# A single-core two-layer gated cross-attention and expert block: the hand-kept order of each engine's steps is replaced by another

## The chip, the cores and the metric

The kernel runs on one NeuronCore of a Trainium2 chip. The metric is the device time of one execution in microseconds (us), the median of several runs. The core has five instruction streams that run side by side and meet at semaphores: PE (TensorE, the matmuls), DVE (VectorE), ACT (ScalarE), POOL (GpSimd) and SP (SyncE, which here issues nearly all DMA transfers).

## The reference

Eight batch elements, each with 256 tokens of 128 numbers (`x`) and a context of 512 tokens of 96 numbers (`ctx`). Four blocks follow each other, each on a layer-normed `x`, with a gate in front of what is added:

```
x = x + tanh(g_xattn[0]) * cross_attention_8_heads_of_64(layernorm(x), ctx)
x = x + tanh(g_ffn[0])   * (self_attention_16_heads_of_8(layernorm(x)) + top2_of_8_experts(layernorm(x)))
x = x + tanh(g_xattn[1]) * cross_attention_16_heads_of_8(layernorm(x), ctx)
x = x + tanh(g_ffn[1])   * top2_of_8_experts(layernorm(x))
```

The four blocks of one batch element depend on each other; the eight elements do not, so the kernel keeps several of them in flight.

## The kernel before

**Stages and steps.** The stages are X (first cross-attention), F (self-attention with the first experts), K (keys and values of the second cross-attention), B (the second cross-attention) and C (the second experts). A step is named by stage, name, batch element b (0 to 7) and a running number k. Nearly every step on PE fills one bank of PSUM, or a pair of banks, and one step on ACT or DVE, the drain, reads it out.

The steps that matter below, with their lines: `ls` (DVE, L1063 and L1066: mean and variance), `rs` (POOL, L1273 and L1274: the reciprocal standard deviation), `xh` (DVE, L1073: normalise), `ln` (PE, L692: transpose, drained by ACT at L923), `qp` (PE L697, two drains on ACT, L937 and L938: queries of X), `kp` (PE L702, ACT L943 and L944: keys of X, two steps for each element), `vp` (PE L708, ACT L947: values of X), `mx` (PE L714, DVE L1105: the largest score of each row of X, eight steps of one wide reduction each), `mT` (PE L720), `e` (PE L730 and L734, ACT L953: scores again and their exponentials), `pv` (PE L743). In stage K, `ctx` (SP L597) loads the context `cTK`, `kk` (PE L772) makes keys and `vv` (PE L826, DVE L1177) values. In F and B, `qk` (PE L765) makes queries (F: and keys), `sp` (POOL L1309 to L1311) splits them into three bf16 parts, `sw` (SP L604, L608) stores the parts to DRAM, `sr` (SP L619, L622) loads them back in another layout (`q8`, `k8`), `mx8` (PE L841 and L847, DVE L1220 and L1225) finds the row maxima, `mT8` (PE L852) transposes them, `mw` and `mr` (SP L652, L657) send them through DRAM into a row of `q8`, and `e8` (PE L866, ACT L996) makes the exponentials, which `pv8` (PE L878) uses.

On POOL there are three steps that occur once: `sets` (L1259, L1262: five memsets of constants into `k8` and `v8`, and two small products that wait until all weights have landed), `bo` (L1251: two bias rows times a gate) and `pick` (L1254: a selection matrix that the first `e` needs). The drains of `vv`, and the loads `sr`, wait for `sets`.

**What sets the order.** The order on each engine is written out in a table, `TURN_OF` (L80 to L105): one string for each engine, in which each letter names a kind of step and takes the next one of that kind. A planner (`schedule`, L332 to L384) walks through these strings, gives each PE step its PSUM banks, and puts filler matmuls (L686) ahead of a PE step where it reckons a long idle time. The instruction streams are then emitted in that order, with a semaphore wait wherever a step needs another engine's. An engine never overtakes: a step that waits holds up all that stands behind it on that engine. For SP this means that a load whose condition is not yet met holds up all later transfers.

**Array shapes on PE.** A step uses the PE array whole, or in halves or quarters of its rows or columns. The table `MODE` (L47 to L50) says which of five shapes a step has (0 whole, 1 row halves, 2 and 3 column halves and quarters, 4 row quarters).

```
MODE = {("X", "mx"): 1, ("X", "e"): 1, ("X", "out"): 1, ("F", "mx8"): 1, ("F", "e8"): 1, ("B", "mx8"): 1, ("B", "e8"): 1,
```

Of the kernel before, what the change touches and what calls it, by code (L numbers as in the profile page):

```python
# [7 lines left out]
ACT = mybir.ActivationFunctionType  # L8
# [81 lines left out]
    "DVE": "abpacccbcccccpdeeccccfcgccchiiikajbkkmkmmmmmmmncdeclecccfgaccchoioqiikrkjkbkmmmmmmmmssnssssssssssssssdtccceclcec"  # L90
           "fcgohoiqciikkrkkplpujuammvmmmmmmsnssswsxsssssssyszsbszszzotAoAcAqccdeerfcgAchcapiuiuicckkkvwxpkmmmmsssssymjmmmnz"
           "sbssszlsssssdzzssAtAeceAccAfcgchocciioqikrkckakmmmpmjmpumlumbssmnsssssssssssssvsdwtxeecycczfcgzzzacAhiAiooiAckqc"
           "ckjrbAkmmmmmumpkupmmnssvswsssssssslssxssstyozozzzdAceecqfAgcrhcAiicAikcckkcpumkmmmsumsspmsmmsnjsssssslsssssvwtdx"
# [1294 lines left out]
```

## Time and profile before

| | before |
|---|---|
| median of 3 runs | 726.27 us (725.82 to 726.75) |
| the profiled execution, its own time | 733.98 us |
| its span, from the first to the last instruction | 732.2 us |
| PE busy | 666.7 us, 91% of the span |
| DVE busy | 515.4 us, 70% |
| ACT busy | 402.4 us, 55% |
| POOL busy | 385.8 us, 53% |
| mean granted TensorE clock | 0.968 of full speed |
| the chain that ended last, by engine | PE 53%, DVE 26%, ACT 6%, POOL 5%, DMA 4% |

Times in the rows are counted from the span's start. An engine's row gives its idle time just before, in brackets, and what ended it. A matmul of fp32 data shows as two records for each instruction, so a step of four matmuls reads as x8. The profiled execution is 7.71 us longer than the median of the runs without a profile, so differences are taken against its own time and then carried over to the median.

### The profile page before, as it was taken

Reading aid. Unit: us, or ns where it says so; the run is one execution under the profiler, and the core shown is the slowest. Engines: PE = TensorE matmul, PEld = TensorE weight load, DVE = VectorE, ACT = ScalarE, POOL = GpSimd, SP = SyncE. Lnnn points to the kernel's source line nnn. Section 1 sums busy time; section 2 is a strip of 40 time slices with the busy share of each in tenths; the row PEclk is TensorE's granted clock in tenths of the full one; section 3 lists DMA queues with packets and bytes.
Section 4 is the critical chain, followed back from the end, with each engine's and each line's share of the span. In section 5 each row is a group of like instructions: output and inputs, shape, how many; then the busy total and the mean of one; then the engine's idle time right before and its main releaser. Section 6 shows DMA issues by size and latency. Waiting matters only on the chain.

```text
span 732.2 us, 14403 instructions
## 1 busy us (share of the span) xinstructions
PE 666.7 (91%) x5766; PEld 347.3 (47%) x5766; DVE 515.4 (70%) x1018; ACT 402.4 (55%) x574; POOL 385.8 (53%) x535
## 2 busy tenths in 40 slices
PE   6898998998989899988999998999999999999984
PEld 4454554543445454543445454546445543544542
DVE  2505658698558965778868889777479979957636
ACT  1464556446734676426673586476744666376540
POOL 5465675781454547563538746573648625234041
PEclk9899999999898999989999999999999989999998
DMA  6040400511091010820145124240060031000000
GB/s 179 22 95 5 101 3 9 119 24 45 10 161 34 2 45 9 168 33 3 46 99 104 54 51 86 56 99 10 1 130 26 20 78 45 1 20 8 2 1 15
DMA packets 58338, 36.92 MB, mean 50 GB/s; under 512 B 4984, under 2 KB 56288, under 8 KB 58272
## 3 DMA queue, kind: packets, MB, share of 16 engines
q1 hardware_dynamic: 57728, 35.74, 22.2%
q8 instruction: 45, 0.74, 0.4%
q10 hardware_dynamic: 544, 0.26, 0.1%
q14 instruction: 21, 0.17, 0.1%
HBM read 21.07 MB, written 14.93 MB: 49 GB/s over the span
## 4 chain that ended last, share of the span: by engine, by line
PE 53%; DVE 26%; ACT 6%; POOL 5%; DMA 4%; issue 3%; SPq 1%; DVEq 0%; POOLq 0%; ACTq 0%
PE psum L878 7%; PE psum L730 6%; PE psum L743 5%; DVE mx8B L1225 5%; DVE mx8F L1220 5%; PE psum L834 5%; PE psum L866 4%; DVE mxA L1105 3%; PE psum L847 2%; PE psum L702 2%; PE psum L803 2%; PE psum L708 2%; ACT probB L996 2%; PE psum L815 2%; PE psum L761 1%
## 5 line engine op out<-in xcount | busy, mean ns | idle before, releaser
L1225 DVE TENSOR_REDUCE mx8B<-psum 128x2 f32<-128x1024 f32 x112 | 131.6, 1216 | 15.1 <-PE psum L847 14.2
L996 ACT ACTIVATE probB<-psum 128x1024 f32<-128x1024 f32 x112 | 110.7, 1028 | 25.5 <-PE psum L866 19.9
L953 ACT ACTIVATE probX<-psum 128x1024 f32<-128x1024 f32 x64 | 65.5, 1023 | 54.8 <-PE psum L734 54.2
L1105 DVE TENSOR_REDUCE mxA<-psum 128x2 f32<-128x1024 f32 x64 | 76.5, 1217 | 25.2 <-PE psum L714 24.9
L1220 DVE TENSOR_REDUCE mx8F<-psum 128x4 f32<-128x1024 f32 x56 | 66.2, 1219 | 21.9 <-PE psum L841 21.5
L730 PE MATMUL psum<-qA,kA 64*128 64x256 f32 x512 | 76.9, 393 | 1.0 <-ACT mrow L926 0.5
L996 ACT ACTIVATE probF<-psum 128x1024 f32<-128x1024 f32 x56 | 56.7, 1026 | 21.1 <-PE psum L866 17.8
L743 PE MATMUL psum<-probX,vX 128*64 128x256 f32 x512 | 63.8, 393 | 0.7 <-ACT probX L953 0.3
L1316 POOL TENSOR_TENSOR prodC<-prodC 128x256 f32<-128x256 f32 x28 | 20.3, 727 | 73.7 <-DVE prodC L1197 73.7
L878 PE MATMUL psum<-probB,v8B 128*9 128x256 f32 x896 | 56.0, 392 | 0.3 <-ACT probB L996 0.2
L1292 POOL TENSOR_TENSOR sums<-probX 128x512 f32<-128x512 f32 x32 | 40.6, 1267 | 21.4 <-ACT probX L953 21.3
L730 PEld LDWEIGHTS psum<-qA,kA 64*128 64x128 f32 x512 | 40.3, 189 | 23.5 <-issue 5.5
L866 PE MATMUL psum<-q8B,k8B 49*128 49x256 bf16 x448 | 43.6, 284 | 5.2 <-ACT probB L996 2.1
L743 PEld LDWEIGHTS psum<-probX,vX 128*64 128x64 f32 x512 | 34.6, 139 | 25.6 <-issue 8.6
L847 PE MATMUL psum<-k8B,q8B 48*128 48x512 bf16 x224 | 41.2, 384 | 6.0 <-DMA q8B<-q_dB 3.3
L1295 POOL TENSOR_TENSOR sums<-sums,probX 128x512 f32<-128x512 f32 x32 | 40.6, 1269 | 10.7 <-ACT probX L953 8.4
L1300 POOL TENSOR_TENSOR sums<-sums 128x512 f32<-128x512 f32 x15 | 19.0, 1267 | 43.5 <-DVE sums L1114 43.5
L1296 POOL TENSOR_TENSOR sums<-sums,probX 128x512 f32<-128x512 f32 x32 | 40.6, 1268 | 2.5
L734 PE MATMUL psum<-mrow,pick 64*128 64x256 bf16 x256 | 35.8, 271 | 0.0
L878 PEld LDWEIGHTS psum<-probB,v8B 128*9 128x9 f32 x896 | 22.4, 92 | 28.1 <-issue 6.7
L866 PEld LDWEIGHTS psum<-q8B,k8B 49*128 49x128 bf16 x448 | 15.5, 97 | 42.5 <-ACT probB L996 12.8
L834 PE MATMUL psum<-weF,xTF 128*128 128x512 f32 x64 | 34.6, 622 | 0.8 <-ACT probB L996 0.5
(254 smaller groups left out, 1368.0 us busy)
## 6 DMA issues: line engine op xcount, KB each, us to landing
k8B<-k_dK SPq DMA_DIRECT2D x14, 384.0 KB, 6.8
k_dK<-partsK SPq DMA_DIRECT2D x7, 384.0 KB, 2.6
q8F<-q_dF SPq DMA_DIRECT2D x14, 192.0 KB, 4.3
k8F<-k_dF SPq DMA_DIRECT2D x14, 192.0 KB, 5.0
q8B<-q_dB SPq DMA_DIRECT2D x14, 192.0 KB, 4.0
k_dK<-partsK SPq DMA_DIRECT2D x7, 256.0 KB, 2.9
cTX<-in_ctxT SPq DMA_DIRECT2D x8, 192.0 KB, 2.6
cTK<-in_ctxT SPq DMA_DIRECT2D x8, 192.0 KB, 2.5
```

The source lines that it names most:

```text
L730: mm(ps[:, 512 * i + SEQ * c:512 * i + SEQ * (c + 1)], kA[half_i, h, (2 * f + c) * P:(2 * f + c + 1) * P], qA[half_i, h, :], start=True, s ...
L743: last = mm(ps[64 * i:64 * i + 64, 0:SEQ], vX[:, c, h * XD:(h + 1) * XD], prob[s][(2 * k + c // 2) % SLOTS[s]][:, o:o + SEQ], start=(c == ...
L834: last = mm(ps, xT[s][:, t * P:(t + 1) * P], we[s][:, f * 512:(f + 1) * 512], start=True, stop=True)
L847: last = mm(ps[:, KV * i:KV * (i + 1)], q8[s][b % TURNS[s]][64 * i:64 * i + KROWS, p, t * P:(t + 1) * P], k8[s][b % TURNS[s]][64 * i:64 * ...
L866: last = mm(ps[:, 512 * i + SEQ * c:512 * i + SEQ * (c + 1)], k8[s][b % TURNS[s]][64 * i:64 * i + MROWS, p, (c0 + c) * P:(c0 + c + 1) * P] ...
L878: last = mm(ps[32 * i:32 * i + D8 + 1, 0:SEQ], v8[s][:, c, h, :], prob[s][(NPAIR * KEYS[s] // SEQ * b + u) % SLOTS[s]][:, o:o + SEQ], star ...
L953: nc.scalar.activation(prob[s][k % SLOTS[s]][:], ps, ACT.Exp, scale=float(XD) ** -0.5).then_inc(done["ACT"], 1)
L996: nc.scalar.activation(prob[s][(units * b + k) % SLOTS[s]][:], ps, ACT.Exp, scale=float(D8) ** -0.5).then_inc(done["ACT"], 1)
L1105: nc.vector.tensor_reduce(mxA[:, t, h:h + 65:64], ps.rearrange("p (i n) -> p i n", i=2), AX.X, ALU.max, negate=True).then_inc(drained, 1)
L1220: nc.vector.tensor_reduce(mx8[s][:, :, 2 * k:2 * k + 2].rearrange("p t i -> p i t"), ps.rearrange("p (i t n) -> p i t n", i=2, t=QT), AX.X ...
L1225: nc.vector.tensor_reduce(mx8[s][:, t, 2 * p:2 * p + 2], ps.rearrange("p (i n) -> p i n", i=2), AX.X, ALU.max, negate=True).then_inc(drain ...
L1292: engine.tensor_tensor(sums[:, h], p[:, :, 0, :], p[:, :, 1, :], ALU.add).then_inc(S["X"]["psum"], 1)
```

## The change

The steps are the same: each engine has as many steps as before, of the same kinds (937 on PE, 571 on DVE, 505 on ACT, 228 on POOL, 104 on SP). Only the five strings of `TURN_OF` differ, nearly everywhere, and with them the banks and the fillers that `schedule` works out. Two lines of the table stand for all:

```
@@ -78,30 +78,30 @@
 TURN_OF = {
-    "POOL": "dacebalffffffffggehijfafffjffffjjkggehlimajfnojffjfjffffkggheimjjjjkonfalfpfffffqqfqmggheqriojjfpnffjfjffakfflqq"
+    "POOL": "acedbalffffffffggehijajffffffffjjkggheimfaojjfffjffljffkgghneiamjjojfffjknpflffffqgghemqqioqrpjjaffjfjffffkfnlqq"
...
-    "SP": "abgaghbibacdefacdjbkeflhmcdaigjkbeflhmacjdngikbeflmhcadijkgbhefnilmacdjgkefbhilnmcjdkgoefnlmhijklngmnnnn",
+    "SP": "bagaghbbacdiefacbdjkeflmhiacdjkgefbhlmacjdnikgbeflhmiacdjgbkefhnlmcdiajkebgfhlmnicdjokengflmhijklngmnnnn",
```

**The start of POOL.** These are POOL's first rows behind the three short memsets, before the change. `veX` and `rstdX` are the step `rs` of element 0, and the memsets of `k8` and `v8` with the two products `bqm` are `sets`:

```order
L1259 MEMSET k8F 128x2048
L1259 MEMSET k8B 128x4096 x2
L1259 MEMSET v8F 128x288
L1259 MEMSET v8B 128x576
L1262 ISA
L1262 TENSOR_SCALAR bqmF<-mask,bqn 128x4
L1262 TENSOR_SCALAR bqmB<-mask,bqn 128x4
L1273 TENSOR_SCALAR veX<-mvX 128x2
L1274 TENSOR_TENSOR rstdX<-veX,nhalf 128x2
L1251 TENSOR_SCALAR boX<-boX,gates 128x128
```

The same place of POOL after the change:

```order
L1273 TENSOR_SCALAR veX<-mvX 128x2
L1274 TENSOR_TENSOR rstdX<-veX,nhalf 128x2
L1251 TENSOR_SCALAR boX<-boX,gates 128x128
L1251 TENSOR_SCALAR boB<-boB,gates 128x128
L1283 TENSOR_TENSOR xbX<-xin,boX 128x256
L1259 MEMSET k8F 128x2048
L1259 MEMSET k8B 128x4096 x2
L1259 MEMSET v8F 128x288
L1259 MEMSET v8B 128x576
L1262 TENSOR_SCALAR bqmF<-mask,bqn 128x4
L1262 TENSOR_SCALAR bqmB<-mask,bqn 128x4
L1254 TENSOR_TENSOR pick<-ident 128x512
```

The step `rs` of element 0, with `bo` and `xb` behind it, has moved ahead of `sets`; `pick` stands behind `sets` now.

**The start of PE.** PE's first steps behind the fillers, before the change (`vp`, `kp`, `ln`, `vv`, `qp`, `kp`, then the first `mx`):

```order
L708 MATMUL psum<-wvx,cTX 128x512 x2
L702 MATMUL psum<-cTX,wkx 128x512 x2
L692 MATMUL psum<-ident,xhX 128x128 x2
L826 MATMUL psum<-wv8B,cTK 128x128 x2
L697 MATMUL psum<-xTX,wqx 128x256 x4
L702 MATMUL psum<-cTX,wkx 128x512 x2
L714 MATMUL psum<-kAb,qAb 128x512 x2
```

The same place of PE after the change:

```order
L702 MATMUL psum<-cTX,wkx 128x512 x2
L692 MATMUL psum<-ident,xhX 128x128 x2
L697 MATMUL psum<-xTX,wqx 128x256 x4
L708 MATMUL psum<-wvx,cTX 128x512 x2
L714 MATMUL psum<-kAb,qAb 128x512 x4
L702 MATMUL psum<-cTX,wkx 128x512 x2
L714 MATMUL psum<-kAb,qAb 128x512 x4
```

The keys, the transpose and the queries have moved ahead of the values, the first two `mx` ahead of the second `kp`, and `vv` behind four `mx`. ACT drains in the matching order (`ln`, `kp`, `qp`, `vp`, `kp`), and DVE reduces six `mx` before its first drain of `vv`, with `ls` of element 1 behind the second.

**SP around the third load of the context for stage K.** Before the change, behind the loads of `q8F` and `k8F` of element 2 (`xin` is x of element 4, `k8B` the keys of B for element 1, `cTK` the context for K of element 2, `q_dB` and `q8B` the queries of B for element 1):

```order
L588 DMA xin<-in_x 128x2x128
L622 DMA k8B<-k_dK 48x8x512 x2
L597 DMA cTK<-in_ctxT 96x512
L604 DMA q_dB<-partsB 128x3x256
L604 DMA q_dB<-partsB 128x2x256
L604 DMA q_dB<-partsB 128x256
L619 DMA q8B<-q_dB 48x8x256 x2
```

The same place of SP after the change:

```order
L604 DMA q_dB<-partsB 128x3x256
L604 DMA q_dB<-partsB 128x2x256
L604 DMA q_dB<-partsB 128x256
L619 DMA q8B<-q_dB 48x8x256 x2
L597 DMA cTK<-in_ctxT 96x512
L652 DMA m_dF<-m8F 16x256
```

`k8B` and `xin` have moved ahead of the stores of element 2's F parts, and `cTK` behind `q8B`. On PE the step `kk` of element 2, which needs this `cTK`, stood 6 steps behind `qk` of B of element 1 and stands 19 steps behind it now.

## Rows read from the trace of the kernel before

**Rows 1.** The page, busy time of PE and its weight loads: share, instructions.

```profile
PE 666.7 (91%) x5766; PEld 347.3 (47%) x5766; DVE 515.4 (70%) x1018; ACT 402.4 (55%) x574; POOL 385.8 (53%) x535
```

**Rows 2.** Stretches: length, busy us of PE, PEld, DVE, ACT, POOL (instructions), PEclk, DMA, GB/s.

```profile
40.00:80.00 40.00, 37.78 (x280) 21.32 (x276) 15.53 (x32) 21.69 (x32) 24.90 (x26) 1.00 0.15 29
...
160.00:200.00 40.00, 36.69 (x343) 16.67 (x344) 28.97 (x41) 28.52 (x38) 12.99 (x17) 0.91 0.06 21
200.00:240.00 40.00, 35.99 (x296) 19.03 (x294) 27.60 (x58) 17.93 (x27) 20.00 (x29) 0.91 0.50 94
...
280.00:320.00 40.00, 34.79 (x253) 17.28 (x253) 24.92 (x56) 19.25 (x33) 26.57 (x41) 0.91 0.53 95
```

**Rows 3.** Timeline of the start: start us, us, engine, line, operation, tiles, count, idle before.

```profile
2.80 6.96 POOL L1259 MEMSET k8B<- 128x4096 bf16 x2
...
5.73 0.25 DVE L1066 BATCH_NORM_AGGREGATE mvX<-st6X 128x2 f32<-128x6 f32 x2
...
13.54 1.88 PE L708 MATMUL psum<-wvx,cTX 96*128 96x512 f32 x4
...
15.26 1.88 PE L702 MATMUL psum<-cTX,wkx 96*128 96x512 f32 x4
...
17.77 0.32 POOL L1262 TENSOR_SCALAR bqmF<-mask,bqn 128x4 f32<-128x4 f32 x1 [7.21 <-DMA weB<-in_weB]
...
18.64 0.72 POOL L1274 TENSOR_TENSOR rstdX<-veX,nhalf 128x2 f32<-128x2 f32 x1
...
19.40 0.65 DVE L1073 TENSOR_SCALAR xhX<-xin,mvX,rstdX 128x128 f32<-128x128 f32 x2 [13.42 <-POOL rstdX L1274]
...
20.20 0.66 PE L692 MATMUL psum<-ident,xhX 128*128 128x128 f32 x2 [3.06 <-DVE xhX L1073]
...
20.90 0.38 ACT L923 ACTIVATE xTX<-psum 128x256 f32<-128x256 f32 x1 [4.41 <-PE psum L692]
21.18 1.02 ACT L943 ACTIVATE kAb<-psum 128x1024 bf16<-128x1024 f32 x1
...
21.51 3.67 PE L697 MATMUL psum<-xTX,wqx 128*128 128x256 f32 x8
...
26.14 1.02 ACT L938 ACTIVATE qA<-psum 128x1024 f32<-128x1024 f32 x1
...
27.41 0.39 PE L714 MATMUL psum<-kAb,qAb 64*128 64x512 bf16 x2
...
27.84 2.36 DVE L1105 TENSOR_REDUCE mxA<-psum 128x2 f32<-128x1024 f32 x2 [3.44 <-PE psum L714]
```

**Rows 4.** The chain that ended last, in order of time: start us, us, what.

```profile
31.84 5.67 DVE mxA L1105 x5
...
501.51 1.73 PE psum L697 x8
```

**Rows 5.** Timeline of PE: two neighbouring steps of different array shape.

```profile
306.13 0.28 PE L734 MATMUL psum<-mrow,pick 64*128 64x256 bf16 x2
306.34 1.95 PE L743 MATMUL psum<-probX,vX 128*64 128x256 f32 x16
```

**Rows 6.** Timelines of SP, then PE, around `kk` of element 2.

```profile
212.11 0.34 SPq L597 DMA_DIRECT2D cTK<-in_ctxT  x1
...
218.16 2.08 PE L772 MATMUL psum<-cTK,wk8B 96*128 96x512 f32 x2 [3.54 <-DMA cTK<-in_ctxT]
...
221.00 1.06 PE L730 MATMUL psum<-qA,kA 64*128 64x256 f32 x4
```

**Rows 7.** Timelines of SP, then PE, around the first `mx8` of B, element 2.

```profile
303.84 1.29 SPq L619 DMA_DIRECT2D q8B<-q_dB  x2
...
315.28 0.61 PE L847 MATMUL psum<-k8B,q8B 48*128 48x512 bf16 x2 [3.28 <-DMA q8B<-q_dB]
...
316.25 3.66 PE L743 MATMUL psum<-probX,vX 128*64 128x256 f32 x16
```

**Rows 8.** Timeline of PE: the first `e8` of B, element 0.

```profile
181.06 0.40 PE L866 MATMUL psum<-q8B,k8B 49*128 49x256 bf16 x4 [1.31 <-DMA q8B<-m_dB]
```

More of the change, by code:

```diff
@@ L90 @@
[L90 to L93, printed above, removed]
-           "eeBfoogqyzrzzhzACiADDiDDikADkDkDkDsjssssussssuspAsssssstvwxylpzooqrzzzAEAFAFFAFFFFFuppuFFFFFvwFFxFyzzzzAAAAuuvwx"
-           "yzzzzGGHGGH",
@@ L101 @@
-    "POOL": "dacebalffffffffggehijfafffjffffjjkggehlimajfnojffjfjffffkggheimjjjjkonfalfpfffffqqfqmggheqriojjfpnffjfjffakfflqq"
-            "ggheimqjojjjaffkfflfqfffrnpggehiqqqamjjqofrjjlfffnfpkfffqggmhqiqojjqjjfffffkefrfflpnghmsoqjjqqjqrpjknmqqqqrnpqqq"
+    "PE": "baceddbddyydxdddexfaggggghghggcbhihjkkdbddedddedldmnpofpggbghgpggaphhsgsgssssbshsiqtcjkkeduduuduvuudvudluvdmddrv"
+          "newowfpggpzgAhpqpgsgsshsgssashsgBBtgBBBBcBbuBuBBBhBuBvBuiBBjuvCudkdubdkDvDdDdDrDuDEvlDDdnwmDpDDEDwpDdDEDdDpozypy"
+          "qEAfFeFgsgsgsssgsessGxHrtBBhBgBhuBuIaBuBvuBguBgBJBvuBBuvBuBhvBgwCbcKhDdDiDDwKDjDEDdDkDkDdEDDKDbDdElDDnmdEdzFKAod"
+          "yFedGpHfpyggpeqpIhsgsgsgsJBBhsgsgsBhBgsBBxbtbBBhBaKuBuiBuBvBuBBBcrKjCdkuevuukvDdDKDduKDdDvEDdDlwDdnmwDEDDdpeDdpD"
+          "DEDozDfApEpyFyFgsgssgshsgsgsBgBxqBsBhBgBGratBgbHBBhBuBhuBiBuBvBBucjCukuvIdkuvuJdDDvDdDbDdlKwmnDEDodDKDEdDKpDDdwq"
+          "pDEDdpeKzDsfAsyDgsEsesgssgspFytFhBgBGxHBBuhBugBuvuBgBrIuBvuBhBuBvugBvaBgBBJbCwcwKihjDdDkDDdDkDEDdDbDdEDdlKmdDnzp"
+          "DdADDEdDDypKfyeEKFpFesgsgsgsgsGsqBBhsgBgBgBshtBHBgBpBhBuoxBuBhBuBvuBiBuvCIjrJukuvukDvDDwDKDwDEDlDKNLznAKDOOoDDEp"
+          "DOpODMKOOEDBDpDBBPqOEBPFBQBByQBBFPRBBQOQBQBBpGBQBRPyCHRQQIxJRDDrDwDwKDDEDDzKSDEUDDKUDDTUEDUDKVUDWUEUWUWUWyVFyFUW"
+          "UWXGUWUWVHUWUWUWXVWIWKJKWWWXKKXFFGHIJYYYY",
@@ new lines @@
+    "DVE": "abccaccccpccbdpececccfcgccchiaiijkkkbkmmmmmmmmndeecccfcgccclhcoioqiirkkajkmmmbkmmmmmssnssssssssssssssdtcecceccfg"
+           "lochiiaiokcqrkkbcpupkujmmmmmmmmvwnslsssxsssssssysssszsztzzoAcoAdceqcefAgcrhccuAjcuapicipivkwxkkbmkmmmyssmmsmsszm"
+           "znszszssAssssssslAtdececAcAfcgcochoqaiciikckrbkupupkjmmmmmmmssssmsnlssssvsswsssssxtdececyfcgzzzozAhcciAiicAjcokq"
+           "krkcAmmmpammmmmpnuuksbsvwsssssxssslssssssytozzzoqzAdcecrecfcgcAhciciikckAAukpumpmmmmmssmssmsnsvswssksxjsssssstdy"
+           "lezeBozfogqzzArAChDjiiiADkDkDDDAskssDsussspsssusDsssksstvwxlpooyqzrzzzEAAFFFFFAFAFFFpupuFFFFvFwFFxyzzzzAAAAuuvwx"
+           "yzzzzGGHGGH",
@@ new lines @@
+    "ACT": "abcdboeafdfffofgffgfcbghgbddijkeffffffbgggaffbglhcdmmmnmmmnminmjkndefpffqlgffgfgfafcmmbgmmnhmnmmbrnrrrmrrsnirrjk"
+           "rrsrrrrsrrpslqedfffftdogfgmmuammnfmfnmvmnmgnfbcrgrrhrrrsrrrrsrrrbrsirrjspqktdeffduglfffgffgfvbbgoammhmnmcmdmnmrr"
+           "rmnrnrsrirrjkrrsrdrrrrprqsesfffgffflogfatfbgmgmhmnmcmmumnnmrrnvrrribjrsrrkrrsrrrrsdplerqrsfdffgftmomgfmnmfummngm"
+           "nmfnafvbhcgrrrrrrsrrbrirsjrkprqrrsrrsdedffffltgffgffgmmomgmmhunnmvmnmrnrrrrrrisrpxqrkrsrrrwsrrrysylzzAyzzztzyAzA"
+           "zuoArrrrvrrrprsrsrrrrBsrrCrDsDDDCDEtDDCDDDCDDuDEvDDDEEtuv",
@@ L103 @@
+    "POOL": "acedbalffffffffggehijajffffffffjjkggheimfaojjfffjffljffkgghneiamjjojfffjknpflffffqgghemqqioqrpjjaffjfjffffkfnlqq"
+            "ggeqhiajmojqffrjfjfkffffplgghnieqjmqqjqoffajrffjpklffnffmgghqeijoqqjqffffjrfffpfnljkgshmoqjqqjqjrjnpkmqqqqrpqqnq"
             "qrpt",
-    "SP": "abgaghbibacdefacdjbkeflhmcdaigjkbeflhmacjdngikbeflmhcadijkgbhefnilmacdjgkefbhilnmcjdkgoefnlmhijklngmnnnn",
+    "SP": "bagaghbbacdiefacbdjkeflmhiacdjkgefbhlmacjdnikgbeflhmiacdjgbkefhnlmcdiajkebgfhlmnicdjokengflmhijklngmnnnn",
```

14 lines of the change are left out of this document (removed).

## Prediction

> **What bounds the kernel now.** I read the page's busy shares first. PE is busy for 91% of the span [rows 1]. Next I read the stretches: from 40 us on PE works 35 to 38 of every 40 us, while DVE works 15 to 29 and ACT 18 to 29 [rows 2]. So from then on the kernel is a queue of PE work with short waits in it, and time is won in three ways: the queue starts earlier, its work gets cheaper, or a wait goes. The same rows show what a long wait costs besides itself: in three of the four stretches the mean granted clock is 0.91, which is 0.09 x 40 = 3.6 us of full-speed PE time lost, since the clock is at 1.2 instead of 2.4 GHz for a part of the stretch. Then I read the timeline of the start. The mean and variance of the first element are ready at 5.73 + 0.25 = 5.98, but POOL's `rs` ends at 18.64 + 0.72 = 19.36, since POOL stands in `sets`, at last until the weights have landed at 17.77 [rows 3]. DVE waits 13.42 us for it and PE 3.06 us, and PE then runs `ln` and `qp` at 1.2 GHz: the 8 records of `qp` take 3.67 us there against 1.73 us at 501.51 [rows 3, 4]. The first `mx` begins on PE at 27.41 and on DVE at 27.84; the eighth ends at 31.84 + 5.67 = 37.51 [rows 3, 4]. Last I looked for the longest waits of PE behind the start: 3.54 us for `cTK` at 218.16 and 3.28 us for `q8B` at 315.28 [rows 6, 7].
>
> **The start.** With `rs` ahead of `sets`, it runs from about 6.0 to 7.1 and `xh` is done before 8 (0.65 us). Now the fillers bound it: PE's first step begins at 13.54 as before, and that is `kp`; the step after it follows at 15.26 [rows 3]. The clock is full by then: the four records of `vp` take 1.88 us. `ln` took 0.66 us at 1.2 GHz, so some 0.4 at 2.4: to 15.7. ACT's copy takes 0.38 us (to 16.1), and PE starts `qp` 0.23 us behind it (21.51 against 20.90 + 0.38), at 16.3; at full clock it lasts 1.73 us, to 18.0. ACT meanwhile drains `kp` in two pieces of 1.02 us, from 16.1 to 18.1, then `qp` in two, to 20.2. The first `mx` follows 0.25 us behind that drain (27.41 against 26.14 + 1.02), at 20.4, and DVE 0.43 us later, at 20.85. That is 7.0 us earlier than 27.84. DVE bounds what follows until the eighth `mx`, and `ls` of element 1, some 0.8 us, now stands among them, so 7.0 - 0.8 = **6.2 us** remain at `mT`. By then PE's order holds the same steps as before, apart from one `ln` that moved behind `mT`. What could be late next: `sets` starts near 9.8, behind `bo` and `xb`, lasts about 9.7 us (its two largest memsets take 6.96) and ends near 20.1, as the weights have landed by 17.77; `pick` ends near 21. The first `e` needs `pick` after 31, and the first drain of `vv` stands behind six `mx`, near 29, so both have 8 us to spare and cost nothing. Without that cover each us of POOL would be a us of PE. Bounds of the start: 3.1 us (PE's wait alone) to 7.0.
>
> **Array shapes.** Two neighbouring PE steps of the same shape overlap by 13.54 + 1.88 - 15.26 = 0.16 us; of different shapes by 306.13 + 0.28 - 306.34 = 0.07 us [rows 3, 5]. A change of shape thus costs 0.09 us. Counted by `MODE` over the 937 steps of PE's order there were 482 changes and are 447, so 35 x 0.09 = 3.2 us of PE time go; PE is busy for 91%, hence **2.9 us** (0 where another engine ends the wait, 3.2 at most).
>
> **Two waits.** `cTK` for element 2 is issued at 212.11 behind 768 KB of `k8B` and PE waits 3.54 us for it [rows 6]. Now `k8B` goes out a whole stage earlier and `cTK` behind `q8B`, so it is issued some 8 us behind `qk`, but `kk` stands 19 steps behind `qk` instead of 6. Work between two steps is counted here and below as the sum of the steps between them in PE's order, each at the median duration that its kind has in this trace. That gives 13.2 us of PE work instead of 3.2, and eight of them are `mx8` of F, which DVE paces at over 1.1 us each. I count the wait as gone. The slow clock behind it took `e`'s first part from 0.6 to 1.06 us [rows 6]; of the stretch's 3.6 us I count 2.8, as part of the slow time fell into the wait. Together **6.3 us** (0 to 7.1). `q8B` of element 2 is issued at 303.84 behind `cTK` and `k8B`, and `mx8` waits 3.28 us [rows 7]. Now `cTK` goes behind it and PE has 22.3 instead of 17.4 us of work between `qk` and `mx8`. The cover grows by 4.9 us, more than the wait, so it goes as well, and with it the slow clock that took `pv` from 1.95 to 3.66 us [rows 5, 7]; I count 2.0 for the clock. Together **5.3 us** (0 to 6.9).
>
> **What is given back.** The trace of before can't show the waits of the new order. It shows what such a place costs: the row transfer of B's maxima held PE 1.31 us at 181.06 [rows 8], and the stretch lost 3.6 us of clock [rows 2], of which I count 3.2, so 4.5 us for the place. Covers have shrunk elsewhere: from `mT8` to `e8` of F there were 9.7 and 10.1 us of PE work for elements 1 and 4 and there are 6.8 and 7.2; of B, element 1, 8.0 and now 6.9, with the stores of K's parts put ahead of the row. I let one new place of 4.5 us come, and 3.1 us of waits too short to touch the clock: **-7.6 us**. Between none and five such places (0 to 22.5) I take the lower side, since the other covers of this kind lie between 5.7 and 7.6 us as before.
>
> **The sum.** 6.2 + 2.9 + 6.3 + 5.3 - 7.6 = 13.1 us off the profiled execution's 733.98, so 720.9; that execution stands 7.71 us above the median 726.27, and I carry the difference over: 726.3 - 13.1 = 713.2 us.
>
> **The rivals.** First, **the start alone**: PE time that is set free turns into waits for DVE and ACT, and as many long waits come as go. Then only the 6.2 us count: 720.1 us. For it: no term but the start is a chain that can be followed to its end in the rows; against it: both long waits have a named transfer that moved. The Trainium skill, Perfetto Trace Analysis, "Identifying the Most-Contended Engine", speaks for it: a high matmul share is no good measure of how near TensorE is to its limit, and the busy share of its weight loads is the better one. By it PE would have half its time to spare, since PEld is at 47% [rows 1], and cheaper PE work would bring little. The long waits that PE's rows show, few between 40 and 80 us (37.78 of 40 busy), speak against that reading here.
>
> Second, **all of it stays**: no new long wait comes, and the whole 20.7 us are kept: 705.6 us. For it: fillers that the planner puts where it reckons a long wait stood at two places within PE's order and stand at none now. Against it: at 181.06 and 315.28 there was no filler, and the waits came.
>
> Third, **slower**: the rows of maxima come late. Each of the 14 trips from `mT8` over `mw` and `mr` to `e8` must fit under the PE work between them. If DVE reads `mT8` 1.5 us late, or `mw` stands behind a store of K's parts, the trip of about 6 us no longer fits, and the place costs 4.5 us. Five places eat the 20.7 us; from there on it is slower. Six cost 27.0 us: 726.3 + 27.0 - 20.7 = 732.6 us. For it: at 181.06 a cover of 5.7 us was too short. Against it: of the 14 trips only this one held PE for over a us before, and most covers are unchanged.
>
> Fourth, **nothing**: the start's gain is lost again within the first element, because POOL's sums or DVE bound it until PE's queue fills. Then it is about 726 us. Against it: between 40 and 80 us POOL works 24.90 and DVE 15.53 of 40 us, PE 37.78 [rows 2].
>
> **How the numbers follow.** The forecast of 713.2 gets 0.52, the start alone 0.21, all of it 0.12, slower 0.09, nothing 0.06. The likeliest is the forecast, with a range of its own from 708 to 718. To hold 8 in 10 the range must reach the start alone, with a little for its bounds (3.1 instead of 6.2 would be 723.2), and most of the way to the second rival: 704 to 722, which leaves out the slower case and nothing. A difference of 0.2% (1.5 us) is about what a measurement of this kernel can tell from no change. Faster by more: 0.52 + 0.21 + 0.12 = 0.85; within: 0.06; slower by more: 0.09.
>
> **What would show it.** In the profile of the changed kernel, `rstdX` should end near 7 us, the first `qp` last 1.7 us, the first `mx` on DVE start near 20.9 and the eighth end near 31.3; POOL's `pick` should end before PE reaches `e`. `kk` of element 2 and the first `mx8` of B of element 2 should begin without a wait for a transfer, and the stretches around them show a clock of 1.00. New stretches with a clock near 0.91 would show what is given back, and the row ahead of each names the wait. The prediction is wrong if `pick` or a drain of `vv` holds PE in the start, if PE's idle time behind 40 us grows by more than some 10 us, or if late rows of maxima show up at several `e8`.

## Result and profile after

The changed kernel takes 701.49 us (median, 700.24 to 702.48) against 726.51 us for the kernel before beside it: a ratio of 0.966 with an interval of [0.963, 0.968], or 25.0 us off. The forecast was 713.2 us with a range of 704 to 722. So the sign is right, and the gain is about twice the forecast and lies outside the range.

The profiled execution of the changed kernel takes 700.24 us, its span 698.4 us. Two rows of its page answer to [rows 1] and to the last line of the table of before: busy us, share of the span and instructions of each engine, and the chain that ended last.

```profile
PE 647.8 (93%) x5762; PEld 341.9 (49%) x5762; DVE 520.7 (75%) x1018; ACT 403.8 (58%) x574; POOL 385.9 (55%) x535
...
PE 53%; DVE 32%; POOL 6%; issue 4%; ACT 3%; DMA 1%; SPq 0%; DVEq 0%; POOLq 0%; ACTq 0%
```

PE is busy for 18.9 us less than in the profiled execution of before, and idle for less too. The stretches that answer to [rows 2], with one more (the columns are those of [rows 2], the granted clock is third from the end):

```profile
40.00:80.00 40.00, 38.34 (x270) 20.98 (x268) 19.07 (x44) 19.12 (x27) 25.14 (x31) 1.00 0.11 30
160.00:200.00 40.00, 37.22 (x410) 18.03 (x410) 31.80 (x66) 28.92 (x41) 15.78 (x24) 1.00 0.33 76
200.00:240.00 40.00, 37.99 (x366) 20.68 (x358) 35.04 (x49) 23.33 (x35) 23.21 (x26) 1.00 0.23 59
280.00:320.00 40.00, 37.13 (x293) 19.60 (x296) 34.02 (x65) 20.16 (x29) 29.32 (x36) 1.00 0.39 70
...
440.00:480.00 40.00, 37.52 (x324) 19.53 (x325) 33.93 (x46) 21.62 (x30) 26.64 (x33) 0.96 0.16 48
```

The three stretches that stood at 0.91 stand at 1.00. Between the start and the last 60 us only the stretch from 440 to 480 falls below 1.00, to 0.96. The timeline of the start, which answers to [rows 3]:

```profile
6.46 0.72 POOL L1274 TENSOR_TENSOR rstdX<-veX,nhalf 128x2 f32<-128x2 f32 x1
...
14.38 1.88 PE L702 MATMUL psum<-cTX,wkx 96*128 96x512 f32 x4
...
16.09 0.38 PE L692 MATMUL psum<-ident,xhX 128*128 128x128 f32 x2
...
16.95 1.99 PE L697 MATMUL psum<-xTX,wqx 128*128 128x256 f32 x8 [0.47 <-ACT xTX L923]
...
19.99 1.04 POOL L1254 TENSOR_TENSOR pick<-ident 128x512 bf16<-128x512 f32 x1
...
21.41 2.36 DVE L1105 TENSOR_REDUCE mxA<-psum 128x2 f32<-128x1024 f32 x2 [13.59 <-PE psum L714]
...
29.19 2.35 DVE L1105 TENSOR_REDUCE mxA<-psum 128x2 f32<-128x1024 f32 x2
```

The first `mx` starts on DVE at 21.41 in place of 27.84, and the eighth ends at 31.54 in place of 37.51, so `mT` stands 5.9 us earlier. The two steps of the long waits, `kk` and the first `mx8` of B of element 2, answer to the PE rows of [rows 6] and [rows 7]. They have no bracket now, which means no idle time ahead of them:

```profile
213.88 1.02 PE L772 MATMUL psum<-cTK,wk8B 96*128 96x512 f32 x2
...
296.70 0.81 PE L847 MATMUL psum<-k8B,q8B 48*128 48x512 bf16 x4
```

**Where the time went.** Executions of the kernel before differ among themselves. I therefore took its profile once more.

> The kernel before, unchanged, profiled a second time. Its first profiled execution took 733.98 us against a median of 726.5, the changed kernel's 700.24 against 701.5, so the two traces differ by 33.7 us and the medians by 25.0. If the long waits and the stretches at 1.2 GHz of the first trace belong to the order of the steps, this one shows the same waits (3.5 us at the third kk, 3.3 us at q8B of the third element), the same five slow stretches behind 160 us and a time near 734. If the slow stretches come and go between executions while the waits stay, it takes about 726 with two or three slow stretches fewer (each some 3 us).

That execution took 723.92 us, with a mean clock of 0.986 where the first profile had 0.968 (733.98 us). Both long waits are there again, while low clock stands at three places behind 160 us where the first profile had five. So, as far as two executions show, the waits belong to the order, and the low clock comes and goes:

```profile
213.71 1.34 PE L772 MATMUL psum<-cTK,wk8B 96*128 96x512 f32 x2 [3.58 <-DMA cTK<-in_ctxT]
...
308.92 0.39 PE L847 MATMUL psum<-k8B,q8B 48*128 48x512 bf16 x2 [2.36 <-DMA q8B<-q_dB]
```

Over the executions of before in three later comparisons, the 11 with a mean clock of 0.976 or less took 731.4 us on average, and the 13 at 0.985 or more 724.5 us. The first profile was thus an execution with more low clock than usual, and the second one is nearer to the typical one. The span is PE's busy time, its idle time and 9.4 us behind its last instruction. Split further by the clock records of the trace (full speed is 2.4 GHz, the low level 1.2; the fourth row is an estimate, the busy time less half of what fell into low clock):

| us | before, first profile | before, second profile | after |
|---|---|---|---|
| span | 732.2 | 722.1 | 698.4 |
| PE busy | 666.7 | 658.0 | 647.8 |
| of it at the low level | 36.7 | 13.6 | 3.2 |
| PE's work, were all of it at full clock | 648.3 | 651.1 | 646.2 |
| PE idle ahead of its instructions | 56.0 | 54.7 | 41.3 |

Against the second profile the span fell by 23.7 us: 13.4 us of waits, 5.2 us of clock ((13.6 - 3.2) / 2) and 4.9 us of work. These three add up to 23.5 us. The work row has a flaw: the clock records of the second profile and of after begin at 13 to 14 us, so the slow fillers of the start count there as full, and in the first profile only some of them do; that is why 648.3 and 651.1 differ with the same instructions. From the end of these fillers to the fillers ahead of the last `ln`, PE's work at full clock is 634.0, 634.8 and 629.3 us. The forecast had all three kinds in it; the experiments ask which of its terms were worth what.

### The profile page after: what moved, and what is told of

It is laid out like the page before. It is cut to its first block, busy times and chain, and to the rows that moved or that the text cites. A ratio compares the mean times of both kernels' runs of the same rounds, so it can differ in the third digit from the quotient of the medians.

```text
span 698.4 us, 14395 instructions
## 1 busy us (share of the span) xinstructions
PE 647.8 (93%) x5762; PEld 341.9 (49%) x5762; DVE 520.7 (75%) x1018; ACT 403.8 (58%) x574; POOL 385.9 (55%) x535
## 4 chain that ended last, share of the span: by engine, by line
PE 53%; DVE 32%; POOL 6%; issue 4%; ACT 3%; DMA 1%; SPq 0%; DVEq 0%; POOLq 0%; ACTq 0%
DVE mx8B L1225 8%; PE psum L730 6%; PE psum L743 6%; PE psum L878 6%; PE psum L834 5%; DVE mxA L1105 3%; PE psum L866 3%; PE psum L708 3%; PE psum L803 3%; DVE mx8F L1220 2%; PE psum L847 2%; PE psum L697 2%; POOL sums L1300 2%; PE psum L702 2%; PE psum L841 2%
## 5 line engine op out<-in xcount | busy, mean ns | idle before, releaser
L996 ACT ACTIVATE probB<-psum 128x1024 f32<-128x1024 f32 x112 | 110.3, 1029 | 15.2 <-PE psum L866 14.7
L730 PE MATMUL psum<-qA,kA 64*128 64x256 f32 x512 | 75.5, 387 | 2.2 <-DVE mx8F L1220 0.6
L743 PE MATMUL psum<-probX,vX 128*64 128x256 f32 x512 | 62.1, 385 | 1.0 <-DVE mx8B L1225 0.7
L878 PE MATMUL psum<-probB,v8B 128*9 128x256 f32 x896 | 53.6, 380 | 0.8 <-DVE prodF L1197 0.4
L866 PE MATMUL psum<-q8B,k8B 49*128 49x256 bf16 x448 | 42.2, 273 | 5.0 <-DMA q8B<-m_dB 1.2
L1316 POOL TENSOR_TENSOR prodF<-prodF 128x256 f32<-128x256 f32 x32 | 23.3, 728 | 34.7 <-DVE prodF L1197 34.7
```

The costliest lines, as they stand in the source:

```text
L730: mm(ps[:, 512 * i + SEQ * c:512 * i + SEQ * (c + 1)], kA[half_i, h, (2 * f + c) * P:(2 * f + c + 1) * P], qA[half_i, h, :], start=True, s ...
L743: last = mm(ps[64 * i:64 * i + 64, 0:SEQ], vX[:, c, h * XD:(h + 1) * XD], prob[s][(2 * k + c // 2) % SLOTS[s]][:, o:o + SEQ], start=(c == ...
L866: last = mm(ps[:, 512 * i + SEQ * c:512 * i + SEQ * (c + 1)], k8[s][b % TURNS[s]][64 * i:64 * i + MROWS, p, (c0 + c) * P:(c0 + c + 1) * P] ...
L878: last = mm(ps[32 * i:32 * i + D8 + 1, 0:SEQ], v8[s][:, c, h, :], prob[s][(NPAIR * KEYS[s] // SEQ * b + u) % SLOTS[s]][:, o:o + SEQ], star ...
L996: nc.scalar.activation(prob[s][(units * b + k) % SLOTS[s]][:], ps, ACT.Exp, scale=float(D8) ** -0.5).then_inc(done["ACT"], 1)
L1316: link("X", engine.tensor_tensor(pr_[:, 0:2 * P], pr_[:, 0:2 * P], pr_[:, 2 * P:], ALU.add))
```

## Experiments

The ratios are to the kernel before in the same comparison; 0.001 is 0.73 us. Where two kernels of different comparisons are set against each other, I subtract their ratios; by the intervals, such a difference is good to about 3 us either way, and to 4 us for e2_rest.

**The parts alone, in the old order.** e1_start is before with the rearranged start: the first 20 steps of PE, 13 of DVE, 7 of ACT and 5 of POOL in the order of after. e2_rest is the counterpart, after with the start of before. PE's part of e1_start:

```diff
-L708 MATMUL psum<-wvx,cTX 128x512 x2
 L702 MATMUL psum<-cTX,wkx 128x512 x2
 L692 MATMUL psum<-ident,xhX 128x128 x2
-L826 MATMUL psum<-wv8B,cTK 128x128 x2
 L697 MATMUL psum<-xTX,wqx 128x256 x4
+L708 MATMUL psum<-wvx,cTX 128x512 x2
+L714 MATMUL psum<-kAb,qAb 128x512 x4
 L702 MATMUL psum<-cTX,wkx 128x512 x2
```

> The kernel before with only the start of the change: the first 20 steps of PE, 13 of DVE, 7 of ACT and 5 of POOL are in the new order, all else in the old. Theory of places (the gain sits at the start, at the two long transfer waits and at the slow clock behind them): 6 us faster than before, about 720.5, and the long waits stay. Rival (the start's gain is only kept by what follows in the new order): within 2 us of before.

> The changed kernel with the start of the kernel before put back (the same steps as in e1_start), all else in the new order. Theory of places: the start is worth 6 us and adds to the rest, so about 707.5 us. Rival: the rest alone gives the 25 us or loses more than 6 of them.

e1_start: 728.47 us, 1.003 [1.000, 1.006], nothing gained. e2_rest: 711.44 us, 0.976 [0.970, 0.982], that is 0.0103 or 7.5 us behind the changed kernel. So the start is worth its term in the new order and nothing in the old one. In the traces `mT` of element 0 stands at 37.55 us in e2_rest and at 31.67 in after, 5.9 us apart; the rest of the 7.5 lies behind the start. The trace of e1_start shows where the gain went in the old order. Matched step by step with the second profile of before (the start of the same matmul in both traces), PE is 5.5 to 7.4 us ahead up to 360 us and 0.8 us behind from 380 on. These are PE's steps of element 5 (`vp`, then two `e`), and the stretch around them:

```profile
370.28 2.08 PE L708 MATMUL psum<-wvx,cTX 96*128 96x512 f32 x2 [1.84 <-ACT probB L996]
...
381.72 0.70 PE L730 MATMUL psum<-qA,kA 64*128 64x256 f32 x4 [0.89 <-ACT probX L953]
...
384.19 0.70 PE L730 MATMUL psum<-qA,kA 64*128 64x256 f32 x4 [0.89 <-ACT probX L953]
...
360.00:400.00 40.00, 35.43 (x269) 17.38 (x269) 24.67 (x53) 15.26 (x23) 23.59 (x31) 0.91 0.47 98
```

None of the three is data that is late. `vp` reads a context that an earlier step had used already. The three wait for a PSUM bank: the planner gives out banks by its own reckoning of when they come free, and with 20 steps moved at the start it chose otherwise for 31 steps far behind it. `vp` got the pair that the exponentials of B were still reading. Waits and clock of this place, 1.84 + 0.89 + 0.89 and 3.4 us, make 7.0 us, more than the start saves. e8_bank tests it: the same order, with the banks of before.

```diff
         when, banks = free_banks(p.wide[fill], bank_free, start)
+        if at["PE"] >= 60:
+            i = int(BANKS_BEFORE[at["PE"] - 60])
+            banks = (i, i + 1)[:1 + p.wide[fill]]
+            when = max(bank_free[j] for j in banks)
```

> This is e1_start with one thing more: from the 61st step on PE, each step fills the bank that the same step had in the order of before (up to one renaming of the banks), in place of the bank that the planner chose anew. The sequence of steps on every engine is that of e1_start. In the trace of e1_start three steps of element 5 wait for a bank: vp at 370.28 for 1.84 us, behind the exponentials of B, and e at 381.72 and 384.19 for 0.89 us each; in before the same steps stand in banks that have long been free and do not wait. The stretch from 360 to 400 us of e1_start has a mean clock of 0.91 (3.4 us of full-speed time), in the trace of before it has 1.00. Theory 'banks': the 6 us that the start saves were eaten there, so the waits and the low clock go and the time falls from 728.5 by 3.6 + 3.4 = 7 us, to about 721.5 (719 to 724). Rival 'absorbed': the start's gain is lost because DVE, ACT and POOL pace the steps that follow, whatever the banks: 728 (726 to 730), with longer waits elsewhere.

It takes 723.95 us, 0.9935 [0.990, 0.997]. That is 0.0095 or 6.9 us better than e1_start, in place of the 7 expected, and the intervals of the two are apart. The time itself is 2.5 us above what was written down; 1.3 of them are the kernel before, which stood at 728.13 in that comparison and at 726.79 in the one of e1_start. The same stretch now:

```profile
360.00:400.00 40.00, 38.34 (x330) 20.62 (x330) 31.65 (x62) 20.57 (x28) 28.80 (x38) 1.00 0.51 113
```

So a hand move in this kernel has a second effect that its diff doesn't show. Counted by the step that a bank held before, the planner also changed 52 steps in e4_q8, 57 in e5_three and 52 in e7_ln, and no run holds the banks there. In e2_rest, e12_kk_back and e13_q8_back it is 18, 12 and 13, nearly all at the moved place itself.

**The two waits removed by hand, in the old order.** e3_kk moves the third `kk` 15 steps later, behind `mx8` and four `e` among others, with its drain on ACT and its split on POOL:

```diff
-L772 MATMUL psum<-cTK,wk8B 128x512
 L887 MATMUL psum<-ident,attB 128x128 x2
...
 L730 MATMUL psum<-qA,kA 128x256 x2
 L734 MATMUL psum<-mrow,pick 128x256 x2
+L772 MATMUL psum<-cTK,wk8B 128x512
```

> The kernel before with kk of the third element 14 steps later on PE (behind the eight F mx8 of that element), its drain later on ACT and its split later on POOL, so that the load cTK has time to land; SP's order is the old one. Theory of places: the 3.5 us wait and the slow clock behind it go: 3.5 to 6.3 us faster than before, 720 to 723. Rival (spread gain: many small waits and the 35 shape changes): the wait at kk goes but another one takes its place, within 1.5 us of before.

It takes 722.94 us, 0.9936 [0.990, 0.997], or 4.7 us off, where the term says 6.3; `kk` has no wait any more:

```profile
222.53 1.12 PE L772 MATMUL psum<-cTK,wk8B 96*128 96x512 f32 x2
```

e4_q8 moves the first five `mx8` of B of element 2 later, the first of them behind seven other steps, `kk` of element 3 nineteen steps later, and the load of `cTK` behind `q8B`; e5_three puts e1_start, e3_kk and e4_q8 together.

```diff
 L841 MATMUL psum<-k8F,q8F 128x256 x4
-L847 MATMUL psum<-k8B,q8B 128x512 x2
...
 L826 MATMUL psum<-wv8F,xTF 128x128 x2
 L841 MATMUL psum<-k8F,q8F 128x256 x4
+L847 MATMUL psum<-k8B,q8B 128x512 x10
```

> The kernel before with the first five B mx8 of the third element moved 8 steps later on PE (and later on DVE), and with the load cTK and the step kk of the fourth element behind the loads of q8B. Theory of places: the 3.3 us wait and the slow clock behind it go: 3.3 to 5.3 us faster than before, 721 to 723. Rival (spread gain): the wait moves, within 1.5 us of before.

> The kernel before with the three single changes together: the new start, kk of the third element later, and the first B mx8 of the third element later. Theory of places: the three add up, 6 + 5 + 4 = 15 us faster, about 711, which leaves 10 of the 25 us to the rest of the new order. If the three places hold the whole gain: about 702. Rival (spread gain): little more than the start, about 719.

e4_q8 is slower: 736.16 us, 1.011 [1.006, 1.016]. The wait for `q8B` is gone, but the last two of the five `mx8`, the gate and the next `mx8` of F wait for DVE now, by 0.56, 0.74, 0.74 and 0.38 us, and the bank wait of `vp` of element 5 is here as well:

```profile
384.46 3.78 PE L708 MATMUL psum<-wvx,cTX 96*128 96x512 f32 x4 [1.84 <-ACT probB L996]
...
360.00:400.00 40.00, 34.44 (x319) 16.37 (x316) 22.87 (x55) 24.02 (x36) 20.73 (x32) 0.91 0.45 94
```

e5_three: 723.41 us, 0.992 [0.988, 0.996], or 5.7 us for three terms that the forecast put at 17.8. Here `vp` has its old banks and neither long wait is left; PE's idle time fell by 5.1 us against the second profile of before, while PE spent 26.7 in place of 13.6 us at the low level. The move of e4_q8 lost time by itself, and the banks changed here too, so these runs don't say which of the two took how much. In the old order hand moves thus return a third of what the rows promise.

**The same terms, undone in the new order.** e12_kk_back and e13_q8_back each put one long wait back into the changed kernel. Their moves on SP and the one on PE that goes with each (`k8B` of the first comes from further up; the drains follow on ACT and DVE). `kk` moves from 19 steps behind `qk` to 5, not from 23 as written down.

```diff
+L622 DMA k8B<-k_dK 48x8x512 x2
+L597 DMA cTK<-in_ctxT 96x512
 L604 DMA q_dB<-partsB 128x3x256
...
 L619 DMA q8B<-q_dB 48x8x256 x2
-L597 DMA cTK<-in_ctxT 96x512
...
+L772 MATMUL psum<-cTK,wk8B 128x512
 L730 MATMUL psum<-qA,kA 128x256 x2
...
 L887 MATMUL psum<-ident,attB 128x128 x2
-L772 MATMUL psum<-cTK,wk8B 128x512
```

```diff
+L597 DMA cTK<-in_ctxT 96x512
 L622 DMA k8B<-k_dK 48x8x512 x2
 L619 DMA q8B<-q_dB 48x8x256 x2
-L597 DMA cTK<-in_ctxT 96x512
...
+L847 MATMUL psum<-k8B,q8B 128x512 x4
 L730 MATMUL psum<-qA,kA 128x256 x2
...
 L830 MATMUL psum<-wgB,xTC 128x8 x2
-L847 MATMUL psum<-k8B,q8B 128x512 x4
```

> The changed kernel with the first of the two long waits put back: kk of element 2 stands 5 steps behind qk on PE again instead of 23 (ACT's drain of it ahead of the first e of element 3), and SP loads k8B of element 1 directly ahead of cTK, ahead of the store of q_dB. Theory 'the terms hold in the new order': PE waits 3 to 4 us for cTK near 205, a stretch of low clock follows (1.7 to 3.4 us), and the time rises by the term of the forecast, 6.3 us, from 701.5 to 707.8 (706 to 710). Rival 'absorbed': the wait comes, but the steps behind it had waits of their own that shrink by as much: 702 to 704.

> The changed kernel with the second of the two long waits put back: on SP the load of cTK for element 3 stands ahead of the loads of k8B and q8B of element 2 again, and the first two mx8 of B of element 2 stand six steps earlier on PE, behind the first mx8 of F of element 3, and as many earlier on DVE. Theory 'the terms hold in the new order': PE waits 2.5 to 4 us for q8B near 300, the stretch loses 1.7 to 3.4 us of clock, and the time rises by the term of the forecast, 5.3 us, to 706.8 (705 to 709). Rival 'absorbed': 702 to 704.

e12_kk_back: 709.42 us, 0.9753 [0.972, 0.978], 0.0097 or 7.1 us above the changed kernel. e13_q8_back: 706.32 us, 0.9706 [0.968, 0.974], 0.0050 or 3.6 us above. The rows of both, each with its stretch:

```profile
210.23 1.97 PE L772 MATMUL psum<-cTK,wk8B 96*128 96x512 f32 x2 [4.96 <-DMA cTK<-in_ctxT]
...
200.00:240.00 40.00, 33.17 (x288) 17.96 (x291) 27.15 (x36) 18.83 (x27) 21.06 (x25) 0.96 0.43 81
```

```profile
296.28 1.03 PE L847 MATMUL psum<-k8B,q8B 48*128 48x512 bf16 x4 [3.03 <-DMA q8B<-q_dB]
...
280.00:320.00 40.00, 34.95 (x252) 19.65 (x252) 31.63 (x63) 16.62 (x22) 27.56 (x37) 0.96 0.42 75
```

Wait and low clock come back where they were expected, and the time with them. Matched step by step with after, PE falls back by 7.8 us at the place of the first and by 3.6 at that of the second, and by next to nothing behind it. The two terms, 6.3 and 5.3, hold in the new order at 7.1 and 3.6.

**Array shapes.** e14_shapes swaps 24 pairs of neighbouring steps on PE in the changed kernel (for instance `oT` and `e`), with banks, fillers and the other engines untouched. PE changes its shape 48 times more.

```diff
-L883 MATMUL psum<-ident,oUB 128x128 x4
 L730 MATMUL psum<-qA,kA 128x256 x2
 L734 MATMUL psum<-mrow,pick 128x256 x2
+L883 MATMUL psum<-ident,oUB 128x128 x4
 L730 MATMUL psum<-qA,kA 128x256 x2
```

> The changed kernel with 24 pairs of neighbouring PE steps swapped, so that PE changes its array shape 495 times instead of 447; banks, fillers, and every other engine's order are those of the changed kernel, and no pair was taken in which either step waits for more than 0.15 us. Theory 'a change costs 0.09 us': 48 changes cost 48 x 0.09 = 4.3 us, and the time rises by 4 us, to 705.5 (704 to 707). Rival 'a change costs nothing that matters': 701.5 (700.5 to 702.5), and the 4 us less of full-clock PE work that the traces of the new order show come from elsewhere.

It takes 714.85 us, 0.9816 [0.979, 0.985], that is 11.6 us above the changed kernel, nearly three times what was expected. The page shows the first part of it:

```profile
PE 656.7 (92%) x5762; PEld 343.3 (48%) x5762; DVE 521.2 (73%) x1018; ACT 403.9 (57%) x574; POOL 385.0 (54%) x535
```

Split as in the table above, PE's work at full clock is 651.6 us, 5.4 more than after, or 0.11 us for each change. Half of (10.2 - 3.2) us, 3.5, is clock. The remaining 5.6 us are idle time of PE, and it arises at the swapped pairs: a step that comes one place later makes its reader one place late. The three add up to 14.5, the difference of the spans being 14.7.

**Is it PE's work that bounds the new order?** e6_pe adds 15 fillers, 6.4 us of PE work, to the changed kernel, spread over its middle, between steps of whole-array shape.

```diff
+for n in FILLED:
+    WARMERS[ORDER["PE"][n]] += 1
```

> The changed kernel with 15 more filler matmuls on PE, spread over the order at places where both neighbours use the whole array; each takes 0.43 us at the full clock, 6.4 us in all. The filler results are not used. If PE's work is what bounds the kernel behind the start: 5 to 6.4 us slower, about 707. If PE has time to spare, as the 49% busy share of its weight loads would have it: under 2 us slower.

706.88 us, 0.9722 [0.968, 0.977], 0.0066 or 4.8 us above the changed kernel. By (1 - clock) x time, some 2.9 us of it are clock (7.8 us against 4.9 at the medians). In the trace 14 of the 15 fillers put PE 0.43 to 0.53 us later at their place, and PE's idle time fell by 2.4 us. So added PE work is not free, but a good third of the 6.4 us went into waits that stood there anyway, and part of what the time shows is clock. By the rule that the forecast cites from the Trainium skill, Perfetto Trace Analysis, "Identifying the Most-Contended Engine", PE would have half its time to spare (PEld 49% on the page) and the fillers would cost next to nothing; the measurement decides, and it lies nearer to the busy share of the matmuls.

**The waits that are left.** After's longest waits behind the start are those of `ln` for DVE. In the view of waits (us in total, times, longest):

```profile
PE psum L692 <- DVE xhF L1073: 3.9, 6, 1.2
...
PE psum L692 <- DVE xhC L1073: 3.4, 4, 1.3
...
PE psum L866 <- DMA q8B<-m_dB: 1.2, 1, 1.2
```

e7_ln puts eight of the `ln` one to three steps later on PE (with the steps that must follow them); the first move stands for all:

```diff
-L714 MATMUL psum<-kAb,qAb 128x512 x2
+L714 MATMUL psum<-kAb,qAb 128x512 x4
 L692 MATMUL psum<-ident,xhF 128x128 x2
-L714 MATMUL psum<-kAb,qAb 128x512 x2
```

> The changed kernel with eight of its ln steps one to three steps later on PE (ACT's drains moved to match), at the places where the trace shows PE waiting 0.7 to 1.3 us for xh. If these waits are what is left to win: the waits shrink by up to 7 us in total and the time falls by 3 to 6 us, to about 697. If what waits for ln is late by as much as PE gains: within 1.5 us of the changed kernel.

707.48 us, 0.972 [0.967, 0.977], 4.7 us above the changed kernel. PE's idle time stays the same, 41.2 against 41.3 us. Six waits of `ln` shrink, by 5.5 us in all, and steps that now come earlier wait 5.1 us more, each for under 0.9 us. How much of that is the changed banks was not separated. Clock is lost on top (17.1 against 3.2 us of PE's busy time at the low level), here at a place with two such waits close together and none over 0.9:

```profile
617.71 1.10 PE L772 MATMUL psum<-cTK,wkx 96*128 96x512 f32 x2 [0.80 <-DMA cTK<-in_ctxT]
...
619.59 0.58 PE L830 MATMUL psum<-wgB,xTC 128*128 128x8 f32 x4 [0.56 <-ACT xTC L923]
...
600.00:640.00 40.00, 37.82 (x346) 18.66 (x350) 28.15 (x67) 24.46 (x34) 8.68 (x15) 0.91 0.03 10
```

**The clock by itself.** e9_fill puts 21 fillers into the nine longest waits of before, e10_more 9 into the five longest of after, e11_both adds those of e9_fill to e8_bank.

```diff
+for fill, n in {("F", "ln", 0, 0): 1, ("F", "ln", 1, 0): 1, ("B", "e8", 0, 0): 2, ("K", "kk", 2, 0): 6, ("F", "e8", 2, 3): 2, ("B", "mx8", 2, 0): 5, ("X", "mx", 7, 5): 1, ("F", "ln", 7, 0): 1, ("C", "ln", 5, 0): 2}.items():
+    WARMERS[fill] += n
```

> Before, with 21 fillers of about 0.43 us more on PE, put ahead of the nine steps that wait longest behind 40 us (6 ahead of kk of element 2, 5 ahead of the first mx8 of B of element 2, 2 each ahead of e8 at 181.06, e8 at 241.80 and ln at 645.25, 1 each at 73.04, 123.81, 538.67 and 591.69). They lie inside the waits, so they neither end a wait earlier nor add to the work that is needed; only PE is not idle in them. Theory 'waits cost clock': the stretches of low clock in the middle of the span (30.6 us of them in the profiled execution of before, 10.2 in e0_again) come from these waits and go: mean clock up from 0.981 to 0.988 or more, time down by about 5 us, to 722 (720 to 724). Rival 'the low clock comes of itself': clock stays near 0.98 and the time at 727 or, as fillers overrun shorter waits, up to 2 us above.

> The changed kernel with 9 fillers more ahead of its five longest waits behind 40 us (2 each ahead of ln at 67.01, ln at 129.13, e8 at 173.90 and ln at 464.69, 1 ahead of ln at 85.17). In its profiled execution one stretch of low clock of 3.4 us follows the wait at 464.69, which costs 1.7 us. Theory 'waits cost clock': that stretch goes, the mean clock is 0.994 to 0.995 in every execution, and the time falls by about 1 us, to 700.5 (699.5 to 701.5). Rival: the steps that waited are ready earlier than thought and the fillers delay them, by up to 0.4 us each: 702.5 to 704.

> e8_bank and e9_fill together: the start of the change, the banks of before, and the 21 fillers ahead of the nine longest waits of before. If start, banks and clock are what the two theories say, the gains add: 727 - 6 (start) - 5 (clock) = 716 (714 to 719). What is then still missing to the changed kernel's 701.5, about 15 us, is the waits themselves that the new order avoids and the cheaper changes of array shape. If either theory falls, the time stays near 721 or above.

In e9_fill the clock does what was expected: its median goes from 0.981 to 0.988, and the stretch around `kk` stands at full clock.

```profile
200.00:240.00 40.00, 37.03 (x329) 20.94 (x330) 28.60 (x53) 18.22 (x27) 23.38 (x31) 1.00 0.45 83
```

The time does not follow: 726.16 us, 0.999 [0.996, 1.002]. PE's idle time fell by only 6.5 us against the second profile, and its full-clock work rose by 12.0. So the low clock does come with the waits, but fillers give back what it costs. e11_both takes 720.61 us, 0.989 [0.986, 0.993], where 716 was expected, 0.0043 or 3.1 us better than e8_bank, with intervals that overlap. e10_more takes 699.84 us, 0.9624 [0.958, 0.966], 0.0032 below the changed kernel; the intervals overlap, so whether it beats it isn't settled.

## Why the prediction was wrong

**What bounds the kernel: right for the most part.** Work added to PE shows in the time (e6_pe), though not all of it, and in part by the clock.

**The start, 6.2 us: right.** `rstdX` ends at 7.18 (forecast: near 7), the first `mx` on DVE starts at 21.41 (20.85), the eighth ends at 31.54 (31.3), `pick` is done at 21.03, long before `e`. One step was off: the fillers ahead of it ran longer at the low level (0.63 us for one, 0.38 at full clock), so `kp` begins at 14.38 in place of 13.54, and `qp` takes 1.99 us in place of 1.73. e2_rest puts the worth at 7.5 us, 5.9 of them at `mT`; the rest is low clock at 74, 166 and 187 us in its profiled execution, which after's doesn't have. That the start alone brings nothing in the old order (e1_start) looked like the first and the fourth rival, but e8_bank shows the banks as the reason.

**Array shapes, 2.9 us: right in kind, too small.** e14_shapes gives 0.11 us of PE time for a change where I read 0.09 from one pair, so 35 changes are 3.9 us. Counted behind the start's fillers, PE's full-clock work is 635.1 us on average in five traces of the old order (634.0 to 636.3: before twice, e1_start, e3_kk, e8_bank) and 629.6 in five of the new (628.7 to 630.2: after, e2_rest, e7_ln, e12_kk_back, e13_q8_back), 5.6 us apart. By the price of e14_shapes, the changes account for 3.7 of them (these traces differ by 34 changes on average). The old orders also hold 1.6 fillers more in their middle on average, some 0.7 us at 0.43 each, which the forecast left out of its sum. About 1 us is not accounted for.

**Two waits, 6.3 and 5.3 us: right.** Both are gone, the stretches stand at 1.00, and put back they cost 7.1 and 3.6 us. Together 10.7 where the forecast had 11.6, which agrees within what these comparisons can tell.

**What is given back, -7.6 us: this step failed.** I let one new place with a long wait come and added 3.1 us of short waits, because covers had shrunk. Late rows of maxima, by which I had priced the place, did not come: the only wait of PE for one is the old one (1.2 us in the view of waits; 1.31 in [rows 8]), and the covers of 6.8 to 7.2 us were enough. New waits did come at other steps. The `ln` at 464.69 waits for 1.33 us, 3.4 us of low clock behind it cost 1.7 more, and in both profiles of before it doesn't wait at all. But what I had left out is larger: old waits other than the two long ones go as well, and I had put them at nothing. Matched step by step behind the start against before's second profile, some 36 us of PE's waits go and some 25 come (one that moves to a neighbouring step counts on both sides). So the sign of the term was wrong: apart from the start and the two long waits, PE's idle time fell by 4.6 us more (13.4 less 2.9 at the start and 5.9 at the two waits). Rows of the view by line, first of before's second profile, then of after (the number behind the second bar is PE's idle time ahead of them):

```profile
L803 PE MATMUL psum<-qA,kA 32*128 32x256 f32 x192 | 26.8, 397 | 1.6 <-ACT probB L983 1.0 <-DVE mx8B L1225 0.4 <-ACT probB L996 0.2
L714 PE MATMUL psum<-kAb,qAb 64*128 64x512 bf16 x128 | 24.4, 383 | 4.2 <-DVE mxA L1105 1.6 <-DVE prodF L1197 0.9 <-ACT qA L938 0.6
L788 PE MATMUL psum<-kAb,qAb 32*128 32x256 bf16 (+1 forms) x64 | 9.3, 327 | 1.9 <-DVE sums L1137 0.7 <-ACT probB L983 0.5 <-DVE prodC L1197 0.5
```

```profile
L803 PE MATMUL psum<-qA,kA 32*128 32x256 f32 x192 | 27.8, 394 | 0.7 <-ACT probB L983 0.6
L714 PE MATMUL psum<-kAb,qAb 64*128 64x512 bf16 x128 | 24.1, 382 | 2.1 <-DVE mxA L1105 1.2 <-ACT qA L938 0.3 <-ACT kA L944 0.2
L788 PE MATMUL psum<-kAb,qAb 32*128 32x256 bf16 (+1 forms) x64 | 9.0, 328 | 0.4 <-DVE sums L1137 0.4
```

The short waits ahead of `mx` and in the last element (L788, L803) are about halved or better, at places that I had not priced; those of `ln` behind the start grew, from 7.7 to 11.0 us. The trace of before shows these waits, but only the order of after decides which of them stay.

**The sum and the rivals.** In the new order the parts measure 7.5 + 3.9 + 7.1 + 3.6 = 22.1 us, against 20.7 for the same four in the forecast; within the error of the comparisons the two sums agree. The rest of the 25.0 is the short waits above and the clock behind them. The outcome is the second rival, "all of it stays" (705.6 us, a chance of 0.12), and 4 us better still. **Carrying over** from the profiled execution was the smaller fault: I read the clock's price from an execution at 0.968, where the typical one is at 0.981, and took its 7.71 us as a fixed offset. By (1 - clock) x time the medians lose 13.8 us to the clock before (0.981) and 4.9 us after (0.993), so 8.9 of the 25 us are clock; the forecast named 4.8 us of it at the two waits and about 3 at the start, and took 3.2 back.

What stays open is which single moves of the new order shortened the short waits; no run took them one by one.

## What to carry to other kernels

Price a loss, like a gain, only by a row: a flat discount for waits that might come took 7.6 of the 20.7 us that this forecast had added up. Where a planner hands out buffers, a step moved by hand changes the buffers of steps far behind it; hold them fast before a part of a change is priced alone, or undo the part in the changed kernel. Take two profiles of the kernel before, and look at the clock of both, before a wait's price is read from one of them.
